# Attention by chunks on one core: four signals of TensorE raised by a drain instead of by the last matmul

## The reference, cut to what matters

```python
def gat_conv(x, src, dst, W, a_src, a_dst, b):
    h = (x @ W).reshape(N, HEADS, HEAD_DIM)
    alpha_s = jnp.einsum('nhc,hc->nh', h, a_src)
    alpha_d = jnp.einsum('nhc,hc->nh', h, a_dst)
    e = alpha_s[src] + alpha_d[dst]
    e = jnp.where(e > 0, e, NEG_SLOPE * e)
    m = jax.ops.segment_max(e, dst, num_segments=N)
    ex = jnp.exp(e - m[dst])
    denom = jax.ops.segment_sum(ex, dst, num_segments=N)
    alpha = ex / (denom[dst] + 1e-16)
    msg = h[src] * alpha[:, :, None]
    out = jax.ops.segment_sum(msg, dst, num_segments=N)
    return out.reshape(N, HEADS * HEAD_DIM) + b
h = gat_conv(x, src, dst, W1, a_src1, a_dst1, b1)
h = jax.nn.elu(h)
out = gat_conv(h, src, dst, W2, a_src2, a_dst2, b2)
```

## Time and profile before

| | us |
|---|---|
| median of 3 runs | 3170.58 |
| lowest and highest | 3165.93 and 3170.78 |
| span of the profiled execution | 3179.1 |
| TensorE busy in it | 1968.0 (62%) |
| VectorE busy | 1545.2 (49%) |
| GpSimd busy | 1402.9 (44%) |
| ScalarE busy | 927.1 (29%) |

### The profile page before, as it was taken

How to read it: one execution, slowest core, us unless ns; L and a number is a source line. 1 busy time by engine, 2 the same in 40 slices (tenths; PEclk the granted TensorE clock), 3 DMA queues, 4 the chain that set the end, 5 groups by cost and what they waited for, 6 DMA issues and landing times.

```text
span 3179.1 us, 37685 instructions
## 1 busy us (share of the span) xinstructions
PE 1968.0 (62%) x10259; PEld 1556.4 (49%) x10259; DVE 1545.2 (49%) x4920; ACT 927.1 (29%) x2035; POOL 1402.9 (44%) x1415
## 2 busy tenths in 40 slices
PE   7998344353367999734555564564365455555599
PEld 6887233243237999623443343443244344344377
DVE  4200133233276555634564564575365555566853
ACT  4443576673013444320111111113011111111432
POOL 1000666666603443245555555513555555553143
PEclk9999676666678999876776766787576776677799
DMA  6444565554238999743344344323333443442000
GB/s 215 187 199 192 171 210 187 193 196 141 87 88 279 353 355 351 240 149 117 104 127 124 100 130 124 100 69 104 109 120 117 117 120 116 119 122 88 1 14 28
DMA packets 207421, 473.85 MB, mean 149 GB/s; under 512 B 33230, under 2 KB 100370, under 8 KB 200750
## 3 DMA queue, kind: packets, MB, share of 16 engines
q0 software_dynamic: 63520, 179.35, 20.0%
q1 hardware_dynamic: 112878, 190.07, 16.7%
q10 hardware_dynamic: 30816, 101.99, 9.0%
HBM read 367.19 MB, written 104.90 MB: 148 GB/s over the span
## 4 chain that ended last, share of the span: by engine, by line
another core or an unknown queue 29%; PE 29%; DVE 27%; issue 10%; DVEq 3%; POOL 1%; DMA 1%; ACT 1%; SPq 0%; POOLq 0%; ACTq 0%
PE banks L421 9%; PE banks L1256 7%; DVE arena L1661 3%; DVE arena L1745 3%; PE banks L1268 3%; DVE arena L825 3%; DVE X L834 2%; DVE arena L1710 2%; DVEq L696 2%; DVEq L699 1%; PE banks L1422 1%; DVE xn L1673 1%; POOL arena L1463 1%; PE banks L2164 1%
## 5 line engine op out<-in xcount | busy, mean ns | idle before, releaser
L1463 POOL DMA_INDIRECT arena<-ht,srcT x784 | 783.7, 1000 | 696.7 <-DVE arena L1745 400.8
L783 POOL DMA_INDIRECT arena<-tr,idx1T x392 | 376.5, 961 | 398.3 <-DMA tr<-arena 207.9
L1572 PE MATMUL banks<-arena,XT 128*128 128x264 f32 x884 | 392.6, 536 | 229.1 <-DVE arena L1745 148.5
L811 PE MATMUL banks<-arena 128*128 x884 | 257.1, 454 | 327.0 <-DVE arena L825 258.1
L811 PEld LDWEIGHTS banks<-arena 128*128 128x128 f32 x884 | 196.2, 229 | 388.0 <-issue 356.1
L1572 PEld LDWEIGHTS banks<-arena,XT 128*128 128x128 f32 x884 | 213.2, 260 | 296.8 <-DVE arena L1745 158.5
L1573 PE MATMUL banks<-arena,XT 128*128 128x264 f32 x884 | 358.0, 496 | 0.0
L1745 DVE TENSOR_TENSOR arena<-arena,nrmT 128x528 f32<-128x528 f32 x442 | 309.9, 703 | 20.8 <-ACT nrmT L1519 12.4
L834 DVE TENSOR_TENSOR X<-X,banks 128x256 f32 x221 | 92.6, 419 | 395.3 <-remote 367.6
L421 PE MATMUL banks<-parts 128*128 128x512 f32 x1200 | 275.1, 391 | 4.7 <-DVE parts L381 4.7
L1573 PEld LDWEIGHTS banks<-arena,XT 128*128 128x128 f32 x884 | 228.5, 259 | 58.8
(11 more groups left out here) (366 smaller groups left out, 3284.0 us busy)
## 6 DMA issues: line engine op xcount, KB each, us to landing
arena<-in_L_ffn_w_dram SPq DMA_DIRECT2D x195, 512.0 KB
tr<-arena SPq DMA_DIRECT2D x50, 1024.0 KB, 3.9
XT<-otd ACTq DMA_DIRECT2D x52, 512.0 KB
arena<-ohd ACTq DMA_DIRECT2D x52, 512.0 KB
arena<-dld ACTq DMA_DIRECT2D x28, 512.0 KB
otd<-arena ACTq DMA_DIRECT2D x28, 512.0 KB
ohd<-arena ACTq DMA_DIRECT2D x28, 512.0 KB
arena<-ht,srcT POOLq DMA_INDIRECT x784
```

The source lines that it names most:

```text
L783: pool.indirect_dma_start(Gr[:, o:o + D], None, TR, bass.IndirectOffsetOnAxis(ap=idx1T[:, q:q + 1], axis=0)).then_inc(d_g[b % NG], 16)
L811: mm = ten.matmul(B[n][:, 0:D], OHr[:, n, h, :], Gr[:, h * D:][:, bass.ds(o, D)], start=(h == 0), stop=(h == 1))
L1463: pool.indirect_dma_start(Gall[:, o:o + ROW], None, HT[L], bass.IndirectOffsetOnAxis(ap=srcT[:, q:q + 1], axis=0)).then_inc(d_g[b % NG], 16)
L1572: ten.matmul(B[n][:, 0:MSG], OH[b][:, 2 * j, :], WG[:, j, 0, :], start=True, stop=False)
```

## The change

The last matmul or transpose of four groups no longer raises the group's semaphore. A drain of TensorE stands behind the group and raises it. `products` keeps its signal on the matmul. No matmul, operand or wait changes.

```diff
@@ scores
                 for n in range(2):
-                    t = ten.transpose(B[7][0:8 * CH, n * P:(n + 1) * P], AS[c % 2][:, n * 8 * CH:(n + 1) * 8 * CH], ident[:, :])
-                t.then_inc(sc_ok, 1)
+                    ten.transpose(B[7][0:8 * CH, n * P:(n + 1) * P], AS[c % 2][:, n * 8 * CH:(n + 1) * 8 * CH], ident[:, :])
+                ten.drain().then_inc(sc_ok, 1)
@@ expand
                 for j in range(CC):
                     t = TB[:, bass.ds(to_.at(c * CH + j // 2), 48)]
-                    mm = ten.matmul(B[4 + j % 2][:, 48 * (j // 2):48 * (j // 2) + 48], OT[b][:, j * P:(j + 1) * P], t,
-                                    start=True, stop=True)
-                return mm
+                    ten.matmul(B[4 + j % 2][:, 48 * (j // 2):48 * (j // 2) + 48], OT[b][:, j * P:(j + 1) * P], t,
+                               start=True, stop=True)
+                ten.drain().then_inc(spread_ok, 1)
@@ back
-                    t = ten.transpose(B[7][:, EW + n * 8 * CH:EW + (n + 1) * 8 * CH], SC[:, n * P:(n + 1) * P],
-                                      ident[0:8 * CH, 0:8 * CH])
-                t.then_inc(back_ok, 1)
+                    ten.transpose(B[7][:, EW + n * 8 * CH:EW + (n + 1) * 8 * CH], SC[:, n * P:(n + 1) * P],
+                                  ident[0:8 * CH, 0:8 * CH])
+                ten.drain().then_inc(back_ok, 1)
@@ maxima
-                    mm = ten.matmul(B[6][:, n:n + 25], OHb[b][:, j, :], SB[:, j, 0:25], start=(j % 2 == 0), stop=(j % 2 == 1))
-                mm.then_inc(mx_ok, 1)
+                    ten.matmul(B[6][:, n:n + 25], OHb[b][:, j, :], SB[:, j, 0:25], start=(j % 2 == 0), stop=(j % 2 == 1))
+                ten.drain().then_inc(mx_ok, 1)
@@ the round
                 if n_on:
-                    expand(n).then_inc(spread_ok, 1)
+                    expand(n)
```

## The result

| | before | changed |
|---|---|---|
| median of 4 runs, us | 3170.68 | 3210.65 |
| lowest and highest | 3165.93, 3171.79 | 3200.95, 3216.79 |
| span of the profiled execution | 3179.1 | 3210.0 |

The changed kernel is slower: ratio 1.0131, 95% interval 1.0115 to 1.0147 (the two medians alone give 1.0126). The forecast was 3032 us, with a range to 3250; the measured time is near the lower price (3202 us) of the rival "the drain is as late as the matmul's signal", which had a chance of 0.20.

The account below looks back on a forecast made before the run. It took TensorE's signals reaching VectorE late during GpSimd's indirect DMAs as the bound. 3179.1 - 150 + 11 = 3040 us of span, less 8.5 us for the median, gave 3032 us; range 2890 to 3250.

Parts of the forecast that it names:

- the drain is as late as the matmul's signal: Rival at `expand` and `back`: late drains hold TensorE, so `products(c, 6, 8)` starts late; 3202 to 3317 us, chance 0.20.
- Whether the drain's signal comes in time while gathers run: Step on `expand`'s drain: took `spread_ok` as prompt during gathers; possible win was nothing or the whole wait.
- A': Chunk of the changed kernel's timeline at the same place of the four-chunk pattern as A; not itself forecast.
- the 150 us: Gain at VectorE's waits with `spread_ok` prompt: mean 3.0 us over 50 chunks, ends 35 and 245 us.
- The slower rival: Late drains make TensorE itself stand before `back` and products; lower price 3202 us, upper 3317 us, chance 0.20.
- A: Largest wait of four successive chunks: L1719 starts 12.0 us after `expand`; forecast gain 2.7 us.
- B: Second-largest wait of four successive chunks: L1719 starts 7.6 us after `expand`; forecast gain 2.4 us.
- C: Third-largest wait of four successive chunks: L1719 starts 3.9 us after `expand`; forecast gain 5.4 us.
- D: Smallest wait of four successive chunks: L1719 starts 1.8 us after `expand`; forecast gain 1.6 us.
- What a drain costs: Four added TensorE drains per chunk: taken as 0.2 us per chunk, 11 us in all, ends 0 and 45 us.
- What is late next: VectorE's wait for `pr_ok` at L1661: would grow from 60.2 us to some 200 to 300 us.
- The first rival: All TensorE signals come in time, `pr_ok` too; a chunk falls to GpSimd's 17.6 us; about 2720 us, chance 0.12.

Follow-up runs that it names:

- probe_seq: Kernel before plus increments of an unawaited semaphore by TensorE's sequencer behind `expand` and `back`; 3207.22 us, kernel before beside it 3211.86 us.
- micro: Changed kernel plus signal-less drains behind every fourth matmul of `expand`, and paired drains behind `expand` and `back`; 3298.92 us.
- the second set: Batch of changed-kernel variants and one with only the scores and maxima drains, against the kernel before, which took 2686.27 us there.
- the third and the fifth: Batches of runs on plain DMAs, 64-row gathers, signal-less drains and gather spacing; kernel before beside them 3168.96 and 3195.97 us.
- after_again: The changed kernel, unaltered, run again beside the kernel before at 2686.27 us; 2699.84 us, ratio 1.0053.

## Why the prediction was wrong

**The step that failed** is "Whether the drain's signal comes in time while gathers run", where I took the first signal as prompt. One of its two reasons was sound: the semaphores are quick, and `probe_seq` shows it for TensorE too (0.06 us). The other was the mistake: "TensorE goes through `back` and the matmuls up to L1573 while the signal of `expand` is out, so the array is not held up". The ends of those rows are modelled, and that the matmuls behind had rows said nothing of whether the one ahead was done. The drain is the witness: in A' it stands for 9.0 us, and `micro` shows the stops between groups of four matmuls, each behind its own drain. So the 150 us that the sum took off for a prompt `spread_ok` were not there.

The Trainium skill, page "PSUM — Partial Sum Buffer", section "Engine vs sequencer instructions", says that an update on an engine instruction fires when that instruction completes, and that a drain waits for an idle engine. The traces agree: L1719 starts 1.7 to 12.0 us behind `expand`'s row in the kernel before and 1.7 to 10.5 us in the changed one (chunks with gathers), and the sequencer's increment is not late. The page "Perfetto Trace Analysis", section "Per-instruction lifecycle: what the profiler-reported window actually captures", says that a matmul's end is an estimate; A' agrees, with a drain that ends 9.0 us behind the end of that row. I had cited both and gave the rows more weight.

**The slower rival** was right in mechanism and in its lower price: 3202 us, measured 3210.65. It was worked out as a loss of 0.4 us per chunk (1.6 us in A, nothing in the others) and 0.2 us for the drains. The mean is right; the places are so only in part. The measure is the time from the end of VectorE's scan (L1673, with which it goes into these waits) to the start of the first late sum (L1661). It is 13.88 us before and 14.31 us in the changed kernel, in the mean of the 50 chunks with gathers: 0.43 us more, 21 us in all. By place in the pattern, 10 chunks each:

| place | worked out | before | changed | difference |
|---|---|---|---|---|
| A | 1.6 | 16.42 | 17.46 | 1.04 |
| B | 0 | 13.55 | 13.13 | -0.42 |
| C | 0 | 15.07 | 14.94 | -0.13 |
| D | 0 | 8.00 | 9.66 | 1.66 |

The other ten don't change (16.39 and 16.36 us). A loses, if less than I worked out, and B wins a little. C is unchanged: its L1661 starts 2.3 to 2.7 us behind the end of the run's last gather in both kernels. It is D that loses most. Timeline of D in the changed kernel:

```profile
1635.92 2.36 PE L1541 MATMUL banks<-arena,XT 128*128 x16 [1.00 <-DVE arena L1614]
...
1641.37 0.47 PE L1548 MATMUL banks<-ident,xn 64*128 64x64 f32 x2 [3.10 <-issue]
...
1642.07 1.22 PE L1572 MATMUL banks<-arena,XT 128*128 128x264 f32 x2 [0.23 <-issue]
1643.08 1.09 PE L1573 MATMUL banks<-arena,XT 128*128 128x264 f32 x2
```

The products start 1642.07 - 1638.28 = 3.8 us behind the end of `expand`'s row, before 1629.88 - 1629.69 = 0.2 us, and a pair takes 1.09 us where it took 0.61. The granted clock of the two stretches, changed and before (us, busy time of PE, PEld, DVE, ACT, POOL, then the clock):

```profile
1642.00:1646.00 4.00, 3.94 (x17) 2.96 (x18) 2.45 (x14) 0.31 (x1) 0.00 (x0) 0.50 0.02 5
```

```profile
1629.80:1632.00 2.20, 2.13 (x10) 1.45 (x9) 0.29 (x1) 0.00 (x0) 1.49 (x2) 1.00 0.47 128
```

In the changed kernel TensorE, whose rows show 3.10 us without a matmul ahead of `back`, runs the products at half of its clock (0.50, the 1.2 GHz level), in the kernel before at full clock. The late start is general: over the 54 rounds of both layers that have these products, they start 6.36 us behind the end of `expand`'s row in the mean, before 0.55 us. The lower clock is at most a part of the loss: L1572 and L1573 together are busy for 12.3 us more (762.9 and 750.6 us), and the mean granted clock of the two attention layers is 0.70 and 0.71 in both kernels. In A and C the products ran at the lower clock before as well (1.09 and 1.08 us for a pair). I had no term for it. In the three last chunks of a layer, where no gather runs, the two layers differ: in the second, chunks are (2979.8 - 2941.8) / 2 = 19.0 us apart at a granted clock of 0.77, before 17.2 us at 0.91; in the first they are (2154.8 - 2119.9) / 2 = 17.4 us apart at 0.91, so there the drains cost next to nothing.

**What a drain costs** (0.2 us per chunk, 11 us, with 0 and 45 as ends): measured alone, where no matmul completes late, 14.2 us, 10 to 18. The estimate of 11 us was near it, but half of what was measured is due to scores and maxima, which I had called covered.

**What is late next** (`pr_ok`, under L1661): it did grow, from 60.2 + 15.6 + 4.8 us to 102.6 + 52.3 us with the issue row below 1 us, not to the 200 to 300 us that I gave. As nothing was won ahead of it, the term of 150 us had nothing to stand on.

**The first rival** (all signals come in time, about 2720 us) had a floor that exists: 2686 us is what the kernel before itself takes where TensorE is not late. The changed kernel beside it takes 18.6 us per chunk, of which GpSimd needs 18.4 us for its 14 gathers. No drain brings it there.

**What stays open.** How an indirect DMA keeps TensorE from completing isn't shown, nor whether the results of the matmuls are late or only the word that they are done. It is longer later in a run and for the later matmuls of `expand`, goes with the distance between gathers and ends with a pause; that looks like something that piles up, but no row shows what. Open too is what differed in the second set. It ran on another chip than the other four sets; the third and the fifth shared one, with 3168.96 and 3195.97 us for the kernel before. The gathers look the same there: in `after_again`, too, the last packet of one is through 2.3 us behind its start. No kernel here had gathers that write elsewhere than to SBUF, or drains together with spaced gathers.

## What to carry to other kernels

A row of a matmul that starts later does not show that an earlier one is done. When a consumer waits for TensorE long behind the end of the row, put a drain (or a sequencer's increment beside the matmul's) behind the group as a probe: if the drain stands as long, the work is late, and no other way to signal it helps. Then look for what holds the engine up; here, long runs of gathers by indirect DMA 1.26 us apart. Breaking the runs into eights won 5.0% (`landed4`), into fours nothing, as the pauses then cost GpSimd as much. Spacing them to 1.45 us, with cover to spare on GpSimd, won 7.3% where TensorE is late. Measure such a version beside the kernel before on more than one chip: where nothing is late, the fills are a pure cost to an engine that is the bound there (14 x 1.45 = 20.3 us per chunk against 18.6), which was not run.

## What the runs showed of the hardware that I had not expected

- The same program takes 3169 to 3212 us in five sets and 2686 us in one. For the changed kernel the spans are 3210.0 and 2697.5 us, 512 us apart. Of that, 69 us lie between the first and the last of the 392 gathers of the relational layer (563.2 and 494.0 us), and 388 us between the first and the last start of L1719 in the two attention layers (1403.3 and 1015.7 us together).
- TensorE completes matmuls up to 13 us late while GpSimd issues indirect DMAs 1.26 us apart, and later in a run more so: the drain behind the last four matmuls of `expand` takes 2.21 us in the median between 8 and 12 us into a run and 3.99 us after that, the one behind the first four 0.19 us (`micro`). It is all done within some 3 us of the end of a run's last gather. Plain DMAs of the same bytes, 0.53 us apart in runs of 8.5 us, do nothing of the sort (0.19 us).
- The sequencer of TensorE goes on meanwhile: its own increments take 0.06 us in the median, and later matmuls get rows.
- A load of registers on GpSimd (`spaced`) adds no distance between gathers; a fill of a 128x128 tile that is waited for adds 0.19 to 0.22 us (1.45 us with one, 1.71 us with two).
